# A graph layer on one core: which four groups of edges take their source rows from a prefetch, and how a range test is written

## The reference, cut to what matters

```python
h = jnp.maximum(_layernorm(x, axis=-1), 0.0)          # x: 6250 nodes x 160
x = x + gnn(h, node_vec1, src, dst, edge_attr_4, edge_attr_10, ...)

# inside gnn, for 206250 edges sorted by dst:
w = relu(edge_attr_10 @ W_fc1 * c1) * c2 @ W_fc2 * c3  # 192 weights for each edge
y0, y1 = l0[edge_src], l1[edge_src]                    # rows of linear(h), gathered by source
m0 = w0 * y0 * e0
m1 = (w1 * y0)[:, :, None] * e1[:, None, :]
m2 = (w2 * e0)[:, :, None] * y1
m3 = w3 * jnp.einsum('eud,ed->eu', y1, e1) * INV_SQRT3
s0, s1, s2, s3 = segment_sum(m0 .. m3, edge_dst) * inv # onto the 6250 nodes
out = self_linear(h) + 0.5 * linear(s0 .. s3)
```

## Time and profile before

| | us |
|---|---|
| median of 3 runs | 2098.49 |
| lowest, highest of them | 2095.70, 2098.89 |
| the profiled execution, its own time | 2094.72 |
| span in its profile | 2093.0 |
| busy: TensorE | 1970.3 (94%) |
| busy: VectorE | 1691.0 (81%) |
| busy: GpSimd | 1565.6 (75%) |
| busy: ScalarE | 352.5 (17%) |
| first and last start of a gather from the table | 67.88, 2077.09 |

### The profile page before, as it was taken

One profiled execution on the slowest core, in us unless ns is written; L12 is line 12 of the kernel. 1 busy time (PEld: TensorE's weight loads), 2 busy tenths in 40 slices (PEclk: granted clock), 3 DMA queues, 4 the chain that ended last, 5 costly groups with the idle time before them and its releaser, 6 DMA issues.

```text
span 2093.0 us, 41996 instructions
## 1 busy us (share of the span) xinstructions
PE 1970.3 (94%) x11562; PEld 1526.1 (73%) x11562; DVE 1691.0 (81%) x4682; ACT 352.5 (17%) x662; POOL 1565.6 (75%) x1638
## 2 busy tenths in 40 slices
PE   7899999999999999999999999999999999999998
PEld 6776877777777777777777777777777777777777
DVE  6788888888888887888888878888888888888887
ACT  6311111111111111111111111111111111111111
POOL 7776777777777777777777777777777777777775
PEclk9899999999999999999999989999999999999998
DMA  6232333333333333333333333333333333233332
GB/s 187 71 73 61 71 73 74 76 73 73 74 74 73 75 73 74 74 73 73 73 76 73 72 75 73 73 75 73 73 74 74 73 73 76 72 73 75 74 74 57
DMA packets 160482, 158.36 MB, mean 76 GB/s; under 512 B 87426, under 2 KB 132390, under 8 KB 160458
## 3 DMA queue, kind: packets, MB, share of 16 engines
q0 software_dynamic: 77376, 132.17, 25.7%
q1 hardware_dynamic: 81800, 24.48, 5.3%
q10 hardware_dynamic: 1282, 1.43, 0.2%
HBM read 149.91 MB, written 8.03 MB: 75 GB/s over the span
## 4 chain that ended last, share of the span: by engine, by line
POOL 32%; issue 26%; DMA 19%; DVE 15%; PE 7%; POOLq 1%; DVEq 0%; ACT 0%; ACTq 0%; SPq 0%
POOL y L423 32%; DMA y<-table,idx 18%; DVE hot L747 5%; DVE msg L728 5%; DVE dot L722 4%; PE ps_w L974 1%; PE ps_s L1019 1%; PE ps_s L1021 1%; PE ps_h L967 1%; PE ps_w L929 1%; DVE dots L717 1%; POOLq L435 0%; PE ps_w L930 0%; PE ps_h L907 0%; DVE span L680 0%
## 5 line engine op out<-in xcount | busy, mean ns | idle before, releaser
L423 POOL DMA_INDIRECT y<-table,idx x1596 | 1516.2, 950 | 500.9 <-issue 438.4
L974 PEld LDWEIGHTS ps_w<-w_fc,hr 100*128 100x128 f32 x3224 | 516.5, 191 | 316.5 <-issue 316.5
L974 PE MATMUL ps_w<-w_fc,hr 100*128 100x192 f32 x3224 | 636.2, 341 | 0.0
L1019 PE MATMUL ps_s<-hot,msg 128*128 128x128 f32 x3216 | 461.3, 288 | 78.1 <-DVE msg L738 75.2
L543 ACT ACTIVATE hr<-ps_h 100x512 f32<-100x512 f32 x403 | 240.6, 597 | 1646.5 <-PE ps_h L967 1646.5
L1019 PEld LDWEIGHTS ps_s<-hot,msg 128*128 128x128 f32 x3216 | 407.0, 196 | 138.3 <-DVE msg L738 137.2
L717 DVE TENSOR_TENSOR dots<-y,attr_sb 128x384 f32<-128x384 f32 (+1 forms) x400 | 223.0, 558 | 290.1 <-DMA y<-table,idx 289.8
L967 PE MATMUL ps_h<-rad,w_fc 10*100 10x512 f32 x806 | 445.5, 632 | 0.3 <-issue 0.3
L1021 PE MATMUL ps_s<-hot,msg 128*128 128x128 f32 x3216 | 436.7, 280 | 0.0
L1021 PEld LDWEIGHTS ps_s<-hot,msg 128*128 128x128 f32 x3216 | 403.3, 197 | 0.0
L807 DVE TENSOR_TENSOR acc<-acc,ps_s 64x32 f32 (+1 forms) x1612 | 324.5, 201 | 46.9 <-PE ps_s L1021 5.9
(11 more groups left out here) (94 smaller groups left out, 555.3 us busy)
## 6 DMA issues: line engine op xcount, KB each, us to landing
y<-table,idx POOLq DMA_INDIRECT x1596, 3.3
rad<-in_radial SPq DMA_DIRECT2D x202, 40.0 KB
xres<-in_x SPq DMA_DIRECT2D x7, 560.0 KB, 5.2
out<-xres SPq DMA_DIRECT2D x49, 80.0 KB
table<-y SPq DMA_DIRECT2D x6, 560.0 KB, 3.6
attr_sb<-in_attr SPq DMA_DIRECT2D x202, 16.0 KB
idx<-in_src SPq DMA_DIRECT2D x200, 4.0 KB, 1.7
dst_i<-in_dst ACTq DMA_DIRECT2D x1, 808.0 KB, 7.2
```

The lines of the kernel that those rows point to most:

```text
L423: nc.gpsimd.indirect_dma_start(out=y[:, j, t, :], out_offset=None, in_=table, in_offset=bass.IndirectOffsetOnAxis(ap=idx[:, j // HALF, col ...
L974: ins = nc.tensor.matmul(ps_w[:, s, t, 0:NW], hr[:, s, t * P:(t + 1) * P], w_fc2[:, :], start=True, stop=True)
L1019: nc.tensor.matmul(ps_s[:, s, 0:4 * W], msg[:, s, t, 0:P], hot[:, s, t, 1:V, :], start=(t == 0), stop=(t == T - 1))
```

## The change

It does three things.

1. The four groups that read `ahead` are groups 7, 12, 17 and 22 (turn 1 place 3, turn 3 place 0, turn 4 place 1, turn 5 place 2) in place of groups 24 to 27. Their indices are loaded by four transfers of four columns on ScalarE's queue in place of one of sixteen. There is no turn without `idx` any more; a half whose group was not gathered waits for the other one's gather alone (`landed_of`). GpSimd skips the four groups.
2. The turns are grouped by pairs that begin at an even turn. GpSimd has turns 0 to 5 written out and one loop; VectorE has pairs 0 to 2 written out and one loop; TensorE and ScalarE have pair 0, a loop over two pairs and a loop over 47. A block is finished four groups earlier than before, block 46 in pair 49, so that the last three groups hold no block. The bounds `least` of the third range test follow that, with one `iota` less.
3. `outside` compares with a tile `bounds`, filled by two memsets on GpSimd, using `tensor_tensor`, where it compared with a constant using `tensor_scalar`.

The diff, cut to its core:

```diff
-AHEAD_TURN = 2 * LAG
+AHEAD_GROUPS = (7, 12, 17, 22)
+AHEAD_TURNS = 6
...
+        bounds = sb("bounds", [P, 3])
...
+        def landed_of(i, j):
+            return sum(n * G + j not in AHEAD_GROUPS for n in range(i)) if isinstance(i, int) else i - 1
...
                     for j in range(HALF * c, HALF * c + HALF):
-                        sp.wait_ge(gathered[j], turns * (16 * T))
+                        landed = landed_of(i, j)
+                        if not isinstance(landed, int) or landed > 0:
+                            sp.wait_ge(gathered[j], landed * (16 * T))
...
+            nc.gpsimd.memset(bounds[:, 0:1], float(W) - 0.5).then_inc(consts, 1)
+            nc.gpsimd.memset(bounds[:, 1:3], -0.5).then_inc(consts, 1)
...
-                with pool.Fori(1, AHEAD_TURN + 1) as n:
+                for i in range(AHEAD_TURNS):
                     for j in range(G):
-                        gather_group(n, j, n - 1, [gathered[j]] * T)
-                with pool.Fori(AHEAD_TURN + 1, TURNS - 2) as n:
+                        if i * G + j not in AHEAD_GROUPS:
+                            gather_group(i, j, i == 0, [gathered[j]] * T)
+                with pool.Fori(AHEAD_TURNS, TURNS - 1) as i:
                     for j in range(G):
-                        gather_group(n, j, n, [gathered[j]] * T)
+                        gather_group(i, j, False, [gathered[j]] * T)
...
-            act.dma_start(ahead_idx[:, :], src[:, AHEAD_TURN * AHEAD:(AHEAD_TURN + 1) * AHEAD]).then_inc(ld_ahead, 16)
+            for n, g in enumerate(AHEAD_GROUPS):
+                act.dma_start(ahead_idx[:, n * T:(n + 1) * T], src[:, g * T:(g + 1) * T]).then_inc(ld_ahead, 16)
...
             def outside():
+                dve.wait_ge(consts, 11)
                 dve.wait_ge(dst_step, 6)
-                nc.vector.tensor_scalar(span[:, 3:4], span[:, 0:1], float(W) - 0.5, None, ALU.is_gt).then_inc(dst_step, 1)
-                nc.vector.tensor_scalar(span[:, 4:6], span[:, 1:3], -0.5, None, ALU.is_lt).then_inc(dst_step, 1)
+                nc.vector.tensor_tensor(span[:, 3:4], span[:, 0:1], bounds[:, 0:1], ALU.is_gt).then_inc(dst_step, 1)
+                nc.vector.tensor_tensor(span[:, 4:6], span[:, 1:3], bounds[:, 1:3], ALU.is_lt).then_inc(dst_step, 1)
...
-                groups(0, 2 * G, 0, first=True)
-                with dve.Fori(1, LAG) as k:
-                    groups(k * 2, 2 * G, k * 2)
-                groups(AHEAD_TURN, G, None)
-                with dve.Fori(LAG, PAIRS - 1) as k:
-                    groups(k * 2 + 1, 2 * G, k * 2, block=k - LAG)
-                groups(TURNS - 2, G + LEFT, TURNS - 3, block=IN_LOOP - 1)
+                for k in range(LAG):
+                    pair(k, k == 0, False)
+                with dve.Fori(LAG, PAIRS) as k:
+                    pair(k, False, True)
```

More of the change, by code:

```diff
@@ L47 @@
 LAG = 3
-AHEAD_TURN = 2 * LAG
-assert AHEAD == G * T
+AHEAD_GROUPS = (7, 12, 17, 22)
+AHEAD_TURNS = 6
+assert AHEAD == len(AHEAD_GROUPS) * T and sorted(g % G for g in AHEAD_GROUPS) == list(range(G))
+assert all(g < AHEAD_TURNS * G for g in AHEAD_GROUPS) and AHEAD_TURNS == 2 * LAG
 IN_LOOP = PAIRS - LAG
@@ L261, in _, with load_half @@
                 load_x(c)
-            def load_half(i, c, first, turns, by_index=True):
+            def load_half(i, c, first):
                 k = i * 2 + c
@@ L748, in weigh, with messages @@
                                         attr_of(j, 0, 4).unsqueeze(3).to_broadcast([P, T, 4, W]), ALU.mult).then_inc(msg_done, 1)
-            def messages(i, j, turns):
+            def messages(i, j):
                 g, s = i * G + j, j % 2
-                rows = y if turns is not None else ahead.rearrange("p (g t) c -> p g t c", t=T)
                 if j % HALF == 0:
@@ L755, in messages @@
                 which(g, s)
-                if turns is not None:
-                    dve.wait_ge(gathered[j], turns * (16 * T) + 16 * T)
-                else:
-                    dve.wait_ge(l_done, NODE_UNITS)
-                edge_dots(j, rows=rows)
+                if isinstance(i, int) and g in AHEAD_GROUPS:
+                    n = AHEAD_GROUPS.index(g)
+                    rows = ahead[:, n * T:(n + 1) * T, :]
+                    dve.wait_ge(l_done, NODE_UNITS)
+                    edge_dots(j, rows)
+                else:
+                    rows = y[:, j, :, :]
+                    dve.wait_ge(gathered[j], landed_of(i, j) * (16 * T) + 16 * T)
+                    edge_dots(j, rows)
                 weigh(g, j, s)
@@ L764, in messages @@
                 dve.wait_ge(fc2_done, g + 1)
[L765 to L766 removed]
+                scalar_products(rows, s)
+                vector_products(rows, s)
                 dve.wait_ge(dot_done, g + 1)
@@ L1041, in windowed, with pair @@
             def windowed():
-                def groups(i, n, first=False, block=None):
-                    for j in range(n):
-                        g = i * G + j
-                        if block is not None and j == 3:
-                            pe.wait_ge(hidt_done, block + (NODE_UNITS + 1))
-                        fc1(i + j // G, j % G)
+                def pair(k, first, finish):
+                    for j in range(2 * G):
+                        g = k * (2 * G) + j
+                        if finish and j == 3:
+                            pe.wait_ge(hidt_done, k - LAG + (NODE_UNITS + 1))
+                        fc1(k * 2 + j // G, j % G)
                         if first and j == 1:
@@ L1051, in groups @@
                             fc2(g - 1, (j - 1) % 2)
[L1052 to L1053 removed]
+                        if finish and j == 2:
+                            turn_block(k - LAG, 0, 1)
                         if j >= 2 or not first:
[L1055 to L1057 removed]
+                            windows(g - 2, j % 2, first and j < 4, k - LAG if finish and j == 7 else None)
+                pair(0, True, False)
                 with pe.Fori(1, LAG) as k:
[L1059 to L1063 removed]
+                    pair(k, False, False)
+                with pe.Fori(LAG, PAIRS) as k:
+                    pair(k, False, True)
+                for j in range(LEFT):
+                    g = (TURNS - 1) * G + j
+                    fc1(TURNS - 1, j)
+                    fc2(g - 1, (g - 1) % 2)
+                    windows(g - 2, g % 2, False)
                 last = EDGE_GROUPS - 1
```

154 lines of the change are left out of this document (69 added, 85 removed).

## The result

| | before | after |
|---|---|---|
| median, first measurement (4 runs each) | 2097.78 | 2080.23 |
| lowest, highest | 2095.70, 2098.89 | 2078.01, 2082.13 |
| the profiled execution, its own time | 2094.72 | 2082.13 |
| span in its profile | 2093.0 | 2080.4 |
| busy: TensorE, VectorE, GpSimd | 94%, 81%, 75% | 94%, 81%, 75% |

The ratio is 0.9916, 95% interval 0.9901 to 0.9931: faster by 0.8%, and 2080.23 lies in the predicted range of 2079 to 2093.5, near its low end. The profiled executions differ by 12.6 us, the two pairs of medians by 17.5 and 8.9; the forecast was 12.2.

A forecast was written before the change was run, and what follows sets the result against it. GpSimd's gathers, 1.25 us each, were taken as the bound, not TensorE. Terms -8.0 + 1.8 - 1.0 - 5.0 = -12.2 us took the median from 2098.49 to 2086.3 us, range 2079 to 2093.5.

The forecast's parts named there:

- The wait for indices, -8.0: GpSimd's gathers: the 8.31 us wait for indices in front of group 28 goes away, -8.0 us.
- The slack at the tight spot: Index loads of halves 4, 7, 9 and 12: indices arrive 0.8 us before GpSimd needs them.
- Slow gathers, +1.8: Early gathers: more are lengthened by VectorE's line 747, +1.8 us (0 to +3).
- Sign (6): GpSimd's row of gathers: 2003 us from first to last; 2009 or more would show the prediction wrong.
- The tail, -1.0: After the last gather: VectorE is no longer late at the last group, -1.0 us (0 to 1.7).
- The test with bounds: VectorE's range test before the gathers: `tensor_tensor` isn't held by GpSimd's memset and takes about 0.14 us, not 6.00.
- the rival of the held reciprocal: VectorE behind the test: the memset holds the 8-element reciprocal, start term 0, total -7.2, 2091.3 us; 14 in 100.
- GpSimd's way through the flag: GpSimd after its memset: reading the flag and branching, put at VectorE's 1.14 us, giving a first gather at 62.1.
- The start, -5.0: Node stage up to the first gather: it moves from 67.88 to 62.9 us, -5.0 (-0.4 to -6.5).
- the forecast's own bound of 61.4: First gather: earliest start, 61.4 us, if ScalarE's 1.5 us of extra issues are absorbed.
- nothing there waits for something that doesn't move, up to the memset: Node stage: the extra index transfers shift everything by just 1.5 us, with the memset's end fixed at 60.92.
- rival of four waits at the queue: SyncE's queue at the skips: pending `attr_sb` delays `idx` four times, +27.8 us at most, 2126; 4 in 100.

The follow-up runs named there:

- e11: Second run of the changed kernel with one strided index transfer and half of the memset on ScalarE: 2077.51 against 2093.93 us for the kernel before, ratio 0.9925.
- e7: Changed kernel with groups 20 to 23 fetched ahead in place of 7, 12, 17 and 22: 2089.91 against 2093.36 us for the kernel before, ratio 0.9984.
- e1: The kernel before, unchanged, run again for a second profile: span 2092.2 us.
- e3: The kernel before with only the test against the tile of bounds: 2086.33 against 2093.96 us, ratio 0.9966.
- e2: The changed kernel, unchanged, run again on another chip: 2085.03 against 2093.93 us for the kernel before, ratio 0.9953.
- e4: Changed kernel with the old `tensor_scalar` comparison back, so groups and pairs alone: 2086.91 against 2093.96 us for the kernel before, ratio 0.996.
- e8: Changed kernel with one strided transfer for the four groups' indices in place of four: 2079.53 against 2093.36 us for the kernel before, ratio 0.9937.
- e5: The kernel before with turn 7's indices loaded at turn 6's place in SyncE's queue: 2091.75 against 2093.96 us, ratio 0.9991.
- e12: Changed kernel with two more small transfers issued by ScalarE, on a chip with a reduced TensorE clock: ratio 0.9957 [0.9906, 1.0009].
- e9: Changed kernel with GpSimd clearing only half of `acc` and ScalarE the rest: 2079.87 against 2093.36 us for the kernel before, ratio 0.9933.
- e6: Changed kernel with line 752's first operand read from a cleared PSUM tile, comparing in place of multiplying: profile span 2081.9 us.

## Why the prediction was right, and where it wasn't

**The wait for indices, -8.0: right.** Waits in front of groups 8, 14, 18 and 24 are 0.30 to 0.47 us. In the six other profiles with these groups and the old line 752 none is over 0.85, and the longest of any gather is 1.23, in front of group 23 (e11). The kernel that keeps four in a row has its long wait (10.09, e7). The slack at the tight spot was forecast as 0.8. In the changed kernel:

```profile
93.38 0.34 SPq L282 DMA_DIRECT2D idx<-in_src  x1
```

With the 2.63 us of the earlier trace rows these indices can be used at 96.0; GpSimd is through with group 6 at 96.74. That is 0.7.

**Slow gathers, +1.8: mechanism right, size right on average.** Less the wait, the early surplus was 4.3, 5.1 and 4.1 in the three profiles with the old groups (before, e1, e3), and 5.5 to 7.8, 6.2 on average, in the seven with the new ones and the old line 752 (after, e2, e4, e8 to e11): +1.7. Of that 1.2 are longer issues and the rest is idle time. The single execution is a matter of luck: the forecast's 15 slow gathers between 100 and 190 us became 16 in one profile of the changed kernel and 7 in the other. The run with PSUM and the count of all profiles show the mechanism. The Trainium skill (SBUF — State Buffer, Who interferes with whom) infers that descriptor generation isn't held up by such operations; 0 of 9 against 21 of 33 inside one line speaks against it. Sign (6) wanted 2003 from first to last gather; it is 2005.9 and 2004.3 in the two profiles of the changed kernel, and 2003.8 on average in the seven, against 2009.6 in the three. The late surplus is 2.8 to 4.5 with the old groups and 1.6 to 6.1 with the new ones, so no difference is shown there, and what moves it isn't known.

**The tail, -1.0: right.** It is 15.9, 13.0, 13.0 and 15.6 in the four profiles with the old loops (before, e1, e3, e5) and 12.1 to 13.3 in the nine with the new ones. VectorE's last group starts 4.34, 2.83, 2.83 and 4.41 us behind the start of the last gather with the old loops and 2.36 to 2.50 in all nine with the new ones. So the lag that the forecast named is gone: 1.2 us between the means, 0.3 to 2.1 between single profiles. The tail falls by 1.9 between the means; for the other 0.7 no cause is shown.

**The test with bounds: right.** 0.15 us under the memset, and the rival of the held reciprocal fell with 0.20. From last take to first gather it was forecast 2.90; 2.73 to 3.51 came where the table decides. GpSimd's way through the flag is hidden: 0.16 us behind the memset, not the 1.14 that VectorE's row suggested.

`std`, forecast near 9.2, came at 8.79 and 9.40. That the clock would not fall behind the test came true, too: its mean from 61 to 65 us is 0.50 to 0.54 in the four profiles in which VectorE was held, and 1.00 in the nine others outside e12, from 56 to 62 us (from 52 to 57 in the first profile of the changed kernel).

**The start, -5.0: the sum is right for the execution that wins the race, and one step is wrong.** The forecast had the last take at 58.4 + 1.5 = 59.9 and the first gather at 62.9; e9, with the same issues, had 59.86 and 62.59. The first profile was better, 56.70 and 61.17, the latter 0.2 us below the forecast's own bound of 61.4, since its node stage took 42.4 us from first to last take where e2, e3 and e6 to e11 took 44.6 to 47.2: TensorE's transposes took 0.27 us there from 15.25 on, and in the kernel before still 0.42 at 20.04, with a granted clock of 1.00 in both:

```profile
15.25 0.27 PE L917 MATMUL ps_h<-ident,hid 128*128 128x128 f32 x1
```

```profile
20.04 0.42 PE L908 MATMUL ps_h<-ident,hid 128*128 128x128 f32 x1
```

What made TensorE quicker sooner isn't settled; no other node stage here was as short. The step that failed is "nothing there waits for something that doesn't move, up to the memset". Line 632 does, on GpSimd's conversions, which wait for `dst_i` and don't move; it costs 6 us at once when it is crossed. I had priced the four transfers as a shift of 1.5 us (it was 0.9 to 1.7), and not asked what else reads SBUF on GpSimd when the shifted work arrives. The Trainium skill (SBUF — State Buffer, Who interferes with whom) has the rule: two SBUF inputs on VectorE contend with a GpSimd operation that reads SBUF. I used it for the memset, where it gave "not held", and not for the casts, where it gives "held"; the rows at 9.95 and 10.74 agree with it in both cases. With -5.0 replaced by +0.5 the sum is -6.7, which is about what the second profile shows (span 2085.8 against 2093.0), though by +0.5 at the start, -4.9 in the row and -2.8 in the tail.

**The sum.** That the two profiles differ by 12.6 where 12.2 was forecast is in part luck: the start gave 6.7 in place of 5.0 and the tail 2.6 in place of 1.0, but the row of gathers only 3.3 in place of 6.2. With the means above the row gives 5.8 and the tail 1.9.

**A rival's sum.** The prediction's rival of four waits at the queue comes to +27.8 and 2126 by adding four waits of 8.0 to the one that the kernel before has. It means three more, so it should be -12.2 + 8.0 + 3 x 8.0 = +19.8, and 2118. No such wait appeared.

**The medians.** 17.5 us in the first measurement and 8.9 in the second. The first is more than all four terms at their best, -8.0 + 0 - 1.7 - 6.5 = -16.2, and no run tells where the rest comes from. Six executions on the second chip took 2078.01, 2081.07, 2084.33, 2085.73, 2087.57 and 2087.88; the one of 2087.57 is known to have lost the race. That the other three above 2084 did too fits a step of 6 us, but only the profiled ones were seen.

## What to carry to other kernels

When a change shifts a stretch of work, even by 1 us, look at what stands still beside it on the engines that share something with it, and note the margin: here a crossing cost the length of the other engine's work, 5 to 6 us, not the shift. A skip in a producer's list of work is worth only as much as the buffers and the queue between it and its consumer can take at once, so spread the skips. And small transfers issued ahead of a critical engine's first instruction are work on the path, about 0.5 us each here (2.08 for four): fetch with one strided transfer what can be fetched so.

## What the runs showed of the hardware

- A VectorE operation that reads two SBUF tiles and GpSimd's work on SBUF held each other up, in both directions. A `scalar_tensor_tensor` of seven elements waited 5.60 and 5.07 us until GpSimd's last integer operation was done. A gather's issue on GpSimd took longer in all of 617 cases in which it started 0.05 us or more inside a `tensor_tensor` of two SBUF tiles with over 0.15 us left, by the rest of that operation less 0.13 us (up to 0.50). Gathers that start within 0.025 us of the operation's start take 0.95.
- The memset, which reads nothing, holds up only the `tensor_scalar` of two elements: 6.00, 4.96, 6.27 and 4.81 us, with its own end as theirs; `tensor_tensor`, the reciprocal of 7 and of 8 elements, `scalar_tensor_tensor` and the `tensor_scalar` of one element aren't held (0.14 to 0.20 us for those of up to eight elements).
- One chip granted TensorE 0.80 to 0.82 of its clock as the mean of every execution, and both kernels took 2.84 to 2.86 ms there.
